# Logits of a recommendation model: seven chunks and nine pairs for nine chunks and eight pairs, tile 1 to 3 on bias rows copied by ScalarE

## What is computed

```python
retrieved   = jnp.mean(item_embeddings[indices], axis=1)       # 512 users, 50 rows of 12500 x 512 each
fused_input = jnp.concatenate([user_rep, retrieved], axis=1)   # 512 x 1024
fused_rep   = fused_input @ W_fuse + b_fuse                    # 512 x 512
logits      = fused_rep @ W_proj + b_proj                      # 512 x 12500
```

## Time and profile before

| | before |
|---|---|
| median of three runs | 310.26 us (309.22 to 312.52) |
| the profiled execution, its own time | 309.87 us |
| its span from first to last instruction | 308.0 us |
| PE busy | 296.9 us, 96% |
| PEld busy | 242.3 us, 79% |
| DVE busy | 248.3 us, 81% |
| ACT busy | 128.1 us, 42% |
| granted TensorE clock | 1.00 |

### The profile page before, as it was taken

How to read it: one execution, slowest core, us unless ns; L and a number is a source line. 1 busy time by engine, 2 the same in 40 slices (tenths; PEclk the granted TensorE clock), 3 DMA queues, 4 the chain that set the end, 5 groups by cost and what they waited for, 6 DMA issues and landing times.

```text
span 308.0 us, 4024 instructions
## 1 busy us (share of the span) xinstructions
PE 296.9 (96%) x1384; PEld 242.3 (79%) x1384; DVE 248.3 (81%) x371; ACT 128.1 (42%) x164; POOL 74.9 (24%) x76
## 2 busy tenths in 40 slices
PE   3999999699999999999999999999999999999995
PEld 1559887498888889888887888888888888888884
DVE  5898998778987836999689989979799797996123
ACT  1104664430010012435375575655846458463310
POOL 4766886787777200000000000000000000000000
PEclk9999999999999999999999999999999999999999
DMA  7999999999996322367538966839677494343315
GB/s 271 337 377 312 358 400 377 409 361 403 291 304 211 107 100 69 130 226 277 198 137 324 318 257 220 313 136 292 240 239 295 146 360 159 135 138 128 131 70 199
DMA packets 32547, 75.13 MB, mean 244 GB/s; under 512 B 4511, under 2 KB 20655, under 8 KB 32528
## 3 DMA queue, kind: packets, MB, share of 16 engines
q1 hardware_dynamic: 25264, 58.06, 52.6%
q0 software_dynamic: 5536, 13.73, 13.6%
q10 hardware_dynamic: 1728, 3.10, 2.6%
HBM read 52.85 MB, written 25.60 MB: 255 GB/s over the span
## 4 chain that ended last, share of the span: by engine, by line
PE 80%; DMA 10%; DVE 6%; issue 1%; ACT 1%; POOL 0%; SPq 0%; POOLq 0%; DVEq 0%; ACTq 0%
PE pair L1137 25%; PE pair L1215 15%; PE pair L1217 15%; PE pair L1218 15%; DMA early<-w_proj 7%; PE pair L1083 4%; PE pair L1123 3%; DMA ring<-item_embeddings,rows 2%; DVE w_lo L833 2%; DVE w_lo L919 1%; DMA early<-w_fuse 1%; DVE pair L796 1%; PE pair L1168 0%; DVE t_sums L908 0%; PE pair L1089 0%
## 5 line engine op out<-in xcount | busy, mean ns | idle before, releaser
L440 POOL DMA_INDIRECT ring<-item_embeddings,rows x56 | 59.8, 1067 | 20.3 <-issue 14.0
L1137 PE MATMUL pair<-w_hi,f_hi 128*128 128x500 f32 x144 | 56.7, 394 | 1.8 <-DVE w_lo L833 1.8
L1137 PE MATMUL pair<-w_lo,f_hi 128*128 128x500 f32 x144 | 56.3, 391 | 0.0
L1137 PE MATMUL pair<-w_hi,f_lo 128*128 128x500 f32 x144 | 56.0, 389 | 0.0
L1215 PE MATMUL pair<-w_hi,s_hi 128*128 128x500 f32 x128 | 49.9, 390 | 0.0
L1217 PE MATMUL pair<-w_lo,s_hi 128*128 128x500 f32 x128 | 49.9, 390 | 0.0
L1218 PE MATMUL pair<-w_hi,s_lo 128*128 128x500 f32 x128 | 49.8, 389 | 0.0
L796 DVE SCALAR_TENSOR_TENSOR pair<-ring,mask,pair 128x512 f32<-128x512 f32 x48 | 36.1, 752 | 3.3 <-DVE pair L810 0.5
L1215 PE MATMUL pair<-w_hi,f_hi 128*128 128x500 f32 x96 | 37.3, 389 | 0.1
L1218 PE MATMUL pair<-w_hi,f_lo 128*128 128x500 f32 x96 | 37.2, 388 | 0.0
L1217 PE MATMUL pair<-w_lo,f_hi 128*128 128x500 f32 x96 | 37.2, 387 | 0.0
(11 more groups left out here) (138 smaller groups left out, 433.2 us busy)
## 6 DMA issues: line engine op xcount, KB each, us to landing
w_raw<-w_proj SPq DMA_DIRECT2D x26, 500.0 KB, 8.1
early<-w_proj SPq DMA_DIRECT2D x24, 500.0 KB, 6.7
logits<-part_out SPq DMA_DIRECT2D x21, 500.0 KB, 3.4
logits<-out_sb SPq DMA_DIRECT2D x28, 250.0 KB, 2.3
logits<-out_sb SPq DMA_DIRECT2D x10, 500.0 KB, 3.0
logits<-out_sb ACTq DMA_DIRECT2D x8, 250.0 KB, 7.0
early<-b_proj SPq DMA_DIRECT2D x8, 250.0 KB, 9.9
s_sum<-b_proj SPq DMA_DIRECT2D x8, 250.0 KB, 6.9
```

The lines of the kernel that those rows point to most:

```text
L440: return nc.gpsimd.indirect_dma_start(out=to, out_offset=None, in_=table, in_offset=bass.IndirectOffsetOnAxis(ap=column, axis=0), **how)
L1137: m = nc.tensor.matmul(ps[:, 0:CHUNK], f[:, t, k, :], w, start=begin, stop=(f is f_lo and k == HK - 1))
```

## The change

`RESIDENT` goes from 8 to 7 and `ROUNDS` (the pairs) from 8 to 9; chunk 8, which was done alone, is gone: 7 + 18 = 25 chunks. The rest follows from it or stands beside it:

- **Bias and results of tiles 1 to 3.** ACT copies a bias row into the PSUM bank before the group (`seed`), PE adds onto it, and ACT copies the result out (`copy_out`); only the last four groups of tile 3 are still evacuated by DVE, with bias rows from a new load (`late_bias`). PE waits for a seed before a group.
- **PE's start.** 16 matmuls of 128x256 on a block of ones, whose result nobody reads, stand ahead of the user's part.
- **Second list.** `pack_list(1)` goes from before tile 0's sum to the start of group 1 of tile 0; with it `list_spots(1)` and `list_rows(1)` go back in DVE's list, behind tile 0's adds and `add_home(0)`.
- **Sorting.** `sort(2)` goes from DVE's head into tile 0's stretch, behind tile 1's fifth add. Tile 1's adds 8 to 10 go ahead of the last half of `split_lo`.
- **The end of tile 3.** DVE makes the sums of blocks in another order; the first pair starts after group (3, 5), and the last group of tile 3 goes inside it.
- **Loads.** SP loads the bias rows as soon as chunk 6 has landed; the pairs' first blocks come in tiles 2 and 3.

```diff
-RESIDENT = 8
-ROUNDS = 8
+RESIDENT = 7
+ROUNDS = 9
...
+BIAS_AT = (4, 5, 6, 7, 0, 1, 2)
+COPIED = 3 * RESIDENT + 3
+WARM = 16
...
-            for b in range(BIAS_SLOTS):
-                if b % HK == 0:
-                    sp.wait_ge(lo_ready, 2 * (RESIDENT - 1 + b // HK))
-                load_bias(b)
-            load_chunk(RESIDENT)
+            sp.wait_ge(w_landed[raw_of(RESIDENT - 1)][1], 16 * raw_uses(RESIDENT - 1))
+            for c in range(RESIDENT):
+                if BIAS_AT[c] >= HK:
+                    sp.wait_ge(lo_ready, 2 * 4)
+                    load_bias(c)
+            for c in range(RESIDENT):
+                if BIAS_AT[c] < HK:
+                    sp.wait_ge(lo_ready, 2 * RESIDENT)
+                    load_bias(c)
...
+            sp.wait_ge(seeded, COPIED - RESIDENT)
+            for j in range(2):
+                load_block(1, 0, j)
+            sp.wait_ge(projected, group_of(TILES - 1, 0) + 1)
+            sp.dma_start(part_out[:, :, :, :].rearrange("p a b n -> p (a b n)").unsqueeze(1),
+                         bp_dram[:, 3 * CHUNK:RESIDENT * CHUNK].unsqueeze(1).to_broadcast([P, 1, 4 * CHUNK]))\
+              .then_inc(late_bias_landed, 16)
+            load_pair_bias(0)
...
+            def copy_out(t, c):
+                g = group_of(t, c)
+                act.wait_ge(projected, g + 1)
+                if g == 0:
+                    act.wait_ge(packed, LISTING)
+                if g >= OUT_SLOTS:
+                    act.wait_ge(out_stored[g % OUT_SLOTS], 16 * (g // OUT_SLOTS))
+                nc.scalar.copy(out_sb[:, g % OUT_SLOTS, :], group_bank(t, c)[:, 0:CHUNK]).then_inc(copied, 1)
...
+            def seed(t, c):
+                act.wait_ge(bias_landed[c], 16)
+                if c == 2:
+                    act.wait_ge(ret_ready, HK * (t + 1))
+                else:
+                    act.wait_ge(copied, group_of(t, c - 3) + 1 if c > 2 else group_of(t - 1, RESIDENT - 2 + c) + 1)
+                nc.scalar.copy(group_bank(t, c)[:, 0:CHUNK], bias[:, BIAS_AT[c], 0:CHUNK]).then_inc(seeded, 1)
...
-            act.wait_ge(packed, LISTING)
+            act.wait_ge(packed, 1)
             split_hi(0)
             split_hi(1)
             mean(0)
...
+            seed(1, 0)
+            fused_hi(1, (0, 1))
+            seed(1, 1)
+            fused_hi(1, (2, 3))
+            seed(1, 2)
+            for c in range(RESIDENT - 3):
+                copy_out(1, c)
+                seed(1, c + 3)
...
+            nc.vector.memset(warm[:, 0:2 * P].bitcast(F32), 1.0).then_inc(warm_ready, 1)
             number()
...
             sort(1)
-            sort(2)
             count_columns()
             list_spots(0)
-            for i in range(4):
+            for i in range(DVE_FIRST):
                 add(0, i)
             list_rows(0)
             list_taken(0)
-            list_spots(1)
-            for i in range(4, DVE_FIRST):
-                add(0, i)
-            bias_lo()
             count_left()
             add_last(0)
+            bias_lo()
             dve.wait_ge(laps_ready, 2)
             add_home(0)
             split_lo(0)
-            list_rows(1)
+            list_spots(1)
             split_lo(1)
...
             add(1, 1)
+            split_lo(2, (0,))
+            list_rows(1)
             list_taken(1)
-            split_lo(2)
+            split_lo(2, (1,))
             add(1, 2)
             add(1, 3)
             split_lo(3)
             add(1, 4)
+            sort(2)
             add(1, 5)
             split_lo(4)
             add(1, 6)
             add(1, 7)
-            split_lo(5)
+            split_lo(5, (0,))
             add_home(1)
-            split_lo(6)
+            split_lo(5, (1,))
+            split_lo(6, (0,))
             for i in range(8, last_add(1) + 1):
                 add(1, i)
-            split_lo(7)
+            split_lo(6, (1,))
...
             def project_resident(t, c, halfway=None):
                 g = group_of(t, c)
-                if t and c < 2:
+                if t and g < COPIED:
+                    pe.wait_ge(seeded, g - RESIDENT + 1)
...
+                elif g == 1:
+                    pack_list(1)
+                elif g == 2:
+                    pe.wait_ge(list_kept, LISTING)
...
+            pe.wait_ge(warm_ready, 1)
+            for x in range(WARM):
+                nc.tensor.matmul(total_ps[:, 0:2 * P], warm[:, 0:P], warm[:, 0:2 * P], start=True, stop=True)
             user_part(0)
...
-            pack_list(1)
             pe.wait_ge(laps_ready, 2)
...
-            for t in range(TILES - 1):
-                project(t, RESIDENT, single_ps[t])
...
-            pe.wait_ge(evacuated, TILES * RESIDENT - RESIDENT)
+            wait_evacuated(pe, group_of(TILES - 1, RESIDENT - 4))
             for i in range(ROUNDS):
```

More of the change, by code:

```diff
@@ L373, in store_pair @@
                   .then_inc(pair_stored[e % OUT_SLOTS], 16)
+            for c in range(RESIDENT):
+                store(1, c)
             for k in range(2):
@@ L625, in seed_c @@
                 else:
-                    act.wait_ge(evacuated, TILES * RESIDENT - RESIDENT + 4)
+                    act.wait_ge(f_ready, HK * TILES)
                 nc.scalar.copy(c_ps[:, :, 0:CHUNK], pair_bias[i % 2][0].unsqueeze(1).to_broadcast([P, 2, CHUNK]))\
                   .then_inc(c_seeded, 1)
+            unit_hi_of(0, B11)
+            copy_out(2, RESIDENT - 2)
+            seed(3, 0)
+            mean(3)
+            copy_out(2, RESIDENT - 1)
+            fused_hi(3, (0, 1))
+            seed(3, 1)
+            fused_hi(3, (2, 3))
+            seed(3, 2)
             s_hi_of(0)
-            split_hi(RESIDENT)
-            unit_hi_of(0, B11)
+            copy_out(3, 0)
             s_hi_of(1)
-            for u in range(T2, UNITS):
+            copy_out(3, 1)
+            unit_hi_of(0, T2)
+            copy_out(3, 2)
+            unit_hi_of(0, B21)
+            unit_hi_of(0, T3)
+            seed_b(0)
+            seed_c(0)
+            for u in (T1, T4, B22):
                 unit_hi_of(0, u)
-            seed_b(0)
+            keep_sum(0, 0)
             unit_hi_of(1, B11)
-            keep_sum(0, 0)
-            seed_c(0)
+            keep_sum(0, 1)
             unit_hi_of(1, T2)
@@ L647, in _ @@
                     keep_sum(i, 0)
-                if not i:
-                    keep_sum(0, 1)
                 if more:
@@ L988, in _ @@
             add(1, 7)
-            split_lo(5)
+            split_lo(5, (0,))
             add_home(1)
-            split_lo(6)
+            split_lo(5, (1,))
+            split_lo(6, (0,))
             for i in range(8, last_add(1) + 1):
                 add(1, i)
-            split_lo(7)
-            for t in range(TILES):
+            split_lo(6, (1,))
+            add_last(2)
+            add_pair(2, 0)
+            add(2, 2)
+            fused_lo(1, (0, 1))
+            add(2, 3)
+            fused_lo(1, (2, 3))
+            add(2, 4)
+            for t in (1, 2):
                 for c in range(RESIDENT):
-                    if t + 1 < TILES and t and c < RESIDENT - 2:
+                    if c < RESIDENT - 1:
                         add(t + 1, AHEAD + 2 * c)
@@ L1031, in _ @@
-                    if t:
-                        evacuate(t, c)
-                    if c == RESIDENT - 1 and t in (1, 2):
-                        fused_lo(t + 1)
-                if t + 2 < TILES:
-                    add(t + 2, 4)
-            unit_lo_of(0, T3)
-            for t in range(TILES):
-                if t == TILES - 1:
-                    t_sum(1, 1)
-                evacuate(t, RESIDENT)
-                if t < 3:
-                    unit_lo_of(0, T1 + t)
+                        if t == 1 and c == 1:
+                            sort(3)
+                    elif t == 1:
+                        add_last(3)
+                        add_pair(3, 0)
+                    else:
+                        unit_lo_of(0, B11)
@@ new lines, in _ @@
+                if t == 1:
+                    fused_lo(2)
+                    add_pair(3, 2)
+                    add(3, 4)
+            f_total(0)
+            fused_lo(3, (0,))
+            s_start(0)
+            fused_lo(3, (1,))
+            s_next(0)
+            fused_lo(3, (2,))
+            s_end(0)
+            fused_lo(3, (3,))
+            t_sum(0, 1)
+            s_lo_of(0)
+            f_total(1)
+            s_start(1)
+            s_next(1)
+            s_end(1)
+            t_sum(0, 2)
```

253 lines of the change are left out of this document (114 added, 139 removed).

## The result

The changed kernel takes 316.3 us (median of four, 314.61 to 317.15), the kernel before 310.27: a ratio of 1.018 [1.014, 1.021]. It is slower by 1.4 to 2.1%, and it lies outside the range of 304.8 to 311.8. The profiled execution takes 315.98 with a span of 314.1, against 309.87 and 308.0.

The account below looks back on a forecast made before the run. PE's matmul count was taken as the bound from 67.45 on, with DVE full before. Gain 7.7 at tile 3's turn less 5.46 gave 2.2: 307.7 profiled, 308.0 predicted median; 8-in-10 range 304.8 to 311.8.

Parts of the forecast that it names:

- the sum's 307.7: Whole kernel: gain of 7.7 at tile 3's turn, less 5.46 for matmuls, taken from the profiled 309.87.
- Matmuls: PE: two groups more behind the turn of tile 3, costing 5.46, so break-even is that turn at 108.54.
- The start: PE's head: unread products give back up to 2.0, hidden by slot 10; F moves by 0 to 1.1.
- F: DVE's first `f_lo` of tile 0: 33.93 before, forecast 33.5, a move of 0.4.
- DVE from F to `add_home(1)`: DVE in tile 0: 18.0 becomes 20.3, with a 0.9 wait at `list_rows(1)`; `home` gather at 54.0.
- T1: PE's first product of tile 1: from 67.45 to 64.7, set by DVE; PE's own work would allow F + 28.3.
- ACT's copies and seeds: ACT: two of 0.56 per group, 1.15 in 2.73, hidden under PE; cost nothing.
- Turn of tile 2: PE asks at T1 + 18.0 = 82.7, waits 0 to 1.6, taken as 0.5: 83.2.
- Turn of tile 3: PE asks at 106.3; last gathers land in 2.3, so no wait and a gain of 7.7.
- the rival: Tile 3's turn: last gathers landing in 5.3 put it at 109.3; 311.0, or 312.4 at late ends; chance 0.22.
- The end of tile 3: DVE's sums and ACT's copies, some 11 each, fit under PE's six groups (16.4); late bias taken as nothing.
- The clock in a wait: PE: a wait brings half speed back, costing 2.0 each: 310.0, or 312 for two; chance 0.06.

Follow-up runs that it names:

- e2: The changed kernel with the loads of the first pair's block (0, 1) behind store (2, 5) in place of (2, 2); 315.51 us, ratio 1.014.
- e8: e1 without the 16 unread products at the start; 311.39 us, ratio 1.004.
- e11: e10 without the 16 unread products at the start; 307.38 us, ratio 0.989.
- e13: e10 with 16 unread products of 128x128 among tile 0's sums, the first 16 kept; 307.36 us, ratio 0.990.
- e5: e1 with the turn into tile 1's slots put ahead of PE's wait for `w_lo`; 314.04 us, ratio 1.012.
- e6: e1 and e2 together on the changed kernel: stores first, second blocks late; 310.97 us, ratio 1.003.
- e1: The changed kernel with stores (3, 0) to (3, 2) ahead of the first pair's bias rows and later block loads on SP; 312.03 us, ratio 1.006.
- e3: The changed kernel with the second list's packing, spots and rows back where they were, packed before tile 0's sum; 314.58 us, ratio 1.014.
- after: The changed kernel itself, against the kernel before; 316.3 us, ratio 1.018.
- e4: The changed kernel with `sort(2)` ahead of `list_rows(1)` in DVE's list; 315.21 us, ratio 1.014.
- e7: e6 plus e5's turn, `sort(2)` among tile 0's adds, and two of tile 1's adds ahead of `list_rows(1)`; 307.92 us, ratio 0.993.
- e10: e7 with `evacuate_pair(0, 0)` ahead of two `unit_lo` of round 1; 308.16 us, ratio 0.991.
- e9: The changed kernel with 12 unread products of 128x500 on PE in the first pair's wait; 314.63 us, ratio 1.014.

## Why the prediction was wrong, step by step

Against the sum's 307.7 the profiled execution has 8.3 more: 1.9 from PE's asking for the turn of tile 3 at 108.2 in place of 106.3, 1.40 of waiting there, 3.00 and 1.56 at the first pair; 0.4 is left. The step that failed most is the one that put the end of tile 3 at nothing.

- **Matmuls: right.** The ledger above is this step.
- **The start: inside its range by luck, with one price missing.** F moved by 0.95, inside 0 to 1.1, and `fuse(0)` by 0.2, but not by the way that I named. Slot 10 went out 0.06 earlier (21.79 for 21.85), not up to 1.09, and SP asked for chunk 2 no sooner (27.73, before 27.69). What changed is that ACT's copy of chunk 2 did not wait (31.58; in the earlier trace rows 32.60 after 0.70 of waiting): the load landed sooner behind its issue in this execution, and in e2 later (copy at 34.51, F at 35.84). Why it did is not shown. That the new wait at the sums is followed by half speed in half of the executions was not in the sum (e8, e11, e13).
- **DVE from F to `add_home(1)`: the mechanism right, the term too small.** The wait at `list_rows(1)` was to be 0.9 and is 1.81, because I tied PE's first product to F (0.4 to 1.2 behind it), and it came 1.94 behind: F moved and PE did not. With these 0.9, and a wait of 0.44 for `f_hi` that the sum lacked, the stretch is 21.5, not 20.3; `home` 54.78, not 54.0.
- **T1: wrong by 2.5 (67.22 for 64.7), and by 3.0 counted from F, which came 0.5 before the 33.5 that I took.** Behind DVE's last half of `split_lo`, which ended 1.1 later than F + 26.2, I counted the last half of group 6 and `fuse(1)`. But in `project` the wait for `w_lo` stands ahead of the turn, so the list's slot and the turn (60.45 to 62.5) came behind it too: 1.81 more (e5 moved T1 by 1.8 against F). The 2.2 were in my sum for PE alone, and I left them out of the sum for DVE.
- **ACT's copies and seeds: right.** Behind T1 PE waits at two places only, the turn of tile 3 and the first pair, and for no seed.
- **Turn of tile 2: right.** PE asked 17.8 behind T1 (18.0) and did not wait (0.5 was taken).
- **Turn of tile 3: the rival came true.** I took 2.3 to landing, "as nothing large is loaded at 103". SP's list puts 1 MB of blocks behind `store(2, 2)`, at 99.7: 6.2, and 1.40 of waiting. e6 removes it.
- **The end of tile 3, "taken as nothing": the largest miss.** I counted the engines' work and the late bias's own landing, not what stands behind it on the queue: the stores, which free the slots that DVE writes. 3.00 of idle time and 1.56 at half speed; e1 gives 4.3 back. Its price stood in no case; without the 4.56 the profiled execution would lie at 311.4, inside the range. The sign that I gave for being wrong here was a late bias row; what was late was a store.
- **The clock in a wait: held at 0.06, and it came true.** The absence of half speed after 0.96 of idle time was a row of one short wait; here 1.40 was followed by none either, but 3.0 by none (e3), 9 (after) and 14 products (e4), in three kernels with the same wait. The Trainium skill (TensorE: Matmul & The Clock Gate, Part 1) says of the start of a kernel that one and the same kernel showed 6, 11 or 14 products at half rate; behind a wait the counts here differ as well.

## What to carry to other kernels

When loads are moved, go down the queue that issues them and ask of every store behind them which buffer it frees and who waits for it: 3.5 MB ahead of one store cost 4.3, nearly as much as two groups of matmuls (5.46). An engine that is brought sooner to a wait gains nothing, and on TensorE it can lose: in many executions here a wait of 2 to 3 us was followed by half speed that cost 1.1 to 2.8, so remove the wait, fill it, or arrive later. Where two chains meet at one point, move both (e7): the turn ahead of `w_lo` alone (e5) only lengthened the wait for the gathers, from 0.97 to 2.25.

## What was not expected of the hardware

Unread products help at one place and harm at another by where they leave PE waiting: at the start of the kernel they went with a loss of 1.1 to 1.6 in half of the executions (e1, e6, e10), in the middle of a wait they kept the clock up, worth 1.56 by the steps (e9). And the same wait for gathers of about 2 us left the clock at 1.00 in the profile of after and at 0.66 in that of e6, and I found nothing in the trace that tells the two apart ahead of it.
